# Mamba layer inside a three-engine scan: rows of B and C fetched by DMA instead of made on TensorE, one quarter of the gate z made during the scan, inputs reordered

## The chip, the cores and the metric

The program runs on one core of one Trainium2 chip. The metric is the device time of one execution in microseconds (us), the median of several runs. Names of engines: PE is TensorE, DVE is VectorE, ACT is ScalarE, POOL is GpSimd, SP is SyncE, which only issues DMAs here.

## The reference

Eight images of 512 patches with a class token ahead of them (513 tokens, 256 features) pass through two layers: attention with a diagonal state-space block and a quantised FFN with a depthwise convolution, then a Mamba block and a quantised gated FFN. The change touches only the Mamba block. With x the normalised input it computes, per image:

```
xv = silu(causal_conv4(W_in[:512] x) + b);  z = W_in[512:] x          # 512 channels, 513 tokens
dt = softplus(W_dt x[:64] + b_dt);  B = W_B x;  C = W_C x              # B, C: 16 rows each
for t:  h = exp(dt_t * A) * h + (dt_t * xv_t) * B_t                    # h: 512 channels x 16 states
        y_t = sum over the 16 states n of h[:, n] * C_t[n]
out = x + W_out (y * silu(z))
```

## The kernel before

Images go in pairs: PAIR = 2 images at a time, TURNS = 4 turns of a hardware loop. Features lie on the 128 partitions and tokens along the free axis, in f32. Each engine has its program written out by hand, with semaphores between them (`sem.wait_ge`), so the order on an engine is the order of the code.

A Mamba stage of one turn has three parts.

**Preparation.** After `layer_norm(3)`, PE makes the products `d` (for dt), `bc` (B and C), `x` and `z`, each 128 channels x 513 tokens (`fill`, L626), in four PSUM slots that are taken in turn; the slot of the product four places back must have been read (`slot_free`, table `readers`). ACT adds biases, makes Abs, Exp and Ln of the softplus and the first tap of the convolution; DVE makes three more taps for each of the 8 tiles (L1438), the rounding step `affine2(big4, mid4)`, and `dt_ready` (L1444); POOL makes the middle of the softplus (L1609, L1612) and dt times x (`dtx_ready`, L1616) for both images. DVE also splits `bc` into three bf16 parts `bcp` (L1414 to L1423), so that a bf16 matmul can spread a row exactly.

**Scan.** 32 steps k, 16 for each image: one state n of all 512 channels (4 tiles of 128 x 512, tokens 1 to 512; token 0 is done apart). Buffers `st(0, k)` hold the input of the scan and then h (3 buffers), `st(1, k)` hold h times C (2 buffers), both in the SBUF tensor `big`. In a step:

- PE spreads row B over the 128 partitions into the PSUM bank `b_psum`, and row C into `c_psum` (L852);
- DVE multiplies 3 tiles (even k) or 2 tiles (odd k) of dt*x, in SBUF, by B out of PSUM (`spread`, L1455); ACT copies the B row to SBUF, and POOL multiplies the other 1 or 2 tiles by that copy (`spread_pool`, L1623);
- ACT makes exp(dt*A) for each tile into one of two PSUM banks (`a_psum`);
- DVE scans the four tiles (L1504: decay from PSUM, input from SBUF);
- POOL multiplies all four tiles of h by row C (L1634, SBUF by SBUF), and PE adds the product into `y_psum` by a matmul with the identity (`add_y`, L873).

Order on DVE: `spread(k + 1)`, then the four scans of k. Order on POOL: the product with C of k (L1634), then `spread_pool(k + 2)`. `hc_ready` tells that the product with C is done, `scanned` that a tile is scanned, `y_summed` that PE has read `st(1, k)`.

**End.** The last step is split between DVE and POOL, `gated` multiplies y by silu(z), and PE projects with `wout`.

Of the kernel before, what the change touches and what calls it, by code (L numbers as in the profile page):

```python
# [23 lines left out]
P = 128  # L24
# [36 lines left out]
SETUP_POOL = 6  # L61
# [29 lines left out]
GU_ORDER = ["G0", "G1"] + [n for c in range(HT - 2) for n in (f"G{c + 2}", f"U{c}")] + [f"U{HT - 2}", f"U{HT - 1}"]  # L91


def plan_fills():
# [32 lines left out]
    each(*[f"d{c}" for c in range(DT)])  # L127
    each("bc")
    each(*[f"x{c}" for c in range(DT)])
    each(*[f"z{c}" for c in range(DT)])  # L130
# [47 lines left out]
def build(nc, x, w, scratch, out):  # L178
    with ExitStack() as ctx:
# [19 lines left out]
        wbc = sb("wbc", [P, KT, 96])  # L199
# [3 lines left out]
        sel = sb("sel", [96, 32], BF16)  # L203
        ones96 = sb("ones96", [96, P], BF16)
        bc0 = sb("bc0", [96, PAIR, 32], BF16)
# [15 lines left out]
        bcp = sb("bcp", [96, PAIR, T + 1], BF16)  # L221
# [35 lines left out]

        def big_un(p):
            o = p * 2 * W8
            return big[:, o:o + KT * T].rearrange("p (c t) -> p c t", c=KT)  # L260

        def big_sq(p):
            o = p * 2 * W8 + KT * T
            return big[:, o:o + KT * T].rearrange("p (c t) -> p c t", c=KT)

        def big4(p, n):
            o = p * 2 * W8 + 2 * KT * T + n * DT * T
            return big[:, o:o + DT * T].rearrange("p (c t) -> p c t", c=DT)

# [30 lines left out]
        def c_row(i):  # L300
            o = 5 * W4 + (i % 2) * S
            return big[:, o:o + S]

        def b_row(i):
            o = 5 * W4 + 2 * S + (i % 2) * S
            return big[:, o:o + S]
# [33 lines left out]
        c_psum = psum[:, 6 * BANK:7 * BANK]  # L340
        b_psum = psum[:, 7 * BANK:8 * BANK]

        def a_psum(j):
            o = (4 + j % 2) * BANK
            return psum[:, o:o + BANK]
# [66 lines left out]
        bc_split = signal("bc_split")  # L412
# [6 lines left out]
        b_spread = signal("b_spread")  # L419
        c_spread = signal("c_spread")  # L420
# [5 lines left out]
        c_copied = signal("c_copied")  # L426
        b_used = signal("b_used")
        b_copied = signal("b_copied")
# [48 lines left out]
        for p in range(PAIR):  # L477
# [23 lines left out]
            for c in range(DT):  # L501
                readers[f"x{c}", p] = (m_tap, 3 * (DT * p + c) + 3)
                readers[f"z{c}", p] = (z_silu, DT * p + c + 1)
                readers[f"d{c}", p] = (sp_pre, DT * p + c + 1)
            readers["bc", p] = (bc_split, 6 * p + 2)
# [10 lines left out]
        def _(sp):  # L516
# [17 lines left out]
            def turn(i, last):  # L534
# [41 lines left out]
                for g in range(NGRP):  # L576
                    stack_max(g)
                    if 1 <= g <= NG:
# [4 lines left out]
                        stack_quarter(g - 1, k_stack, K_PARTS, 2)  # L583
                if not last:
                    sp.wait_ge(q_ready, 4 * PAIR)
                    load_x(i + 1)
# [18 lines left out]
        def _(pe):  # L605
# [3 lines left out]
            with pe.Fori(0, TURNS) as i:  # L609
# [220 lines left out]
                for p in range(PAIR):  # L830
                    pe.wait_ge(ln_normed, q_of(3, p))
                    for c in range(DT):
                        fill(f"d{c}", p, [(wdt[:, c * P:(c + 1) * P], big_un(p)[:, 0])])
                for p in range(PAIR):
                    fill("bc", p, [(wbc[:, k], big_un(p)[:, k]) for k in range(KT)], rows=96)
                for p in range(PAIR):
                    for c in range(DT):
                        fill(f"x{c}", p, [(wx[:, k, c * P:(c + 1) * P], big_un(p)[:, k]) for k in range(KT)])
                for p in range(PAIR):
                    for c in range(DT):  # L840
                        fill(f"z{c}", p, [(wz[:, k, c * P:(c + 1) * P], big_un(p)[:, k]) for k in range(KT)])


                pe.wait_ge(z_silu, DT * PAIR)
                pe.wait_ge(bc_split, 6 * PAIR)
                pe.wait_ge(bc_first, 1)
                nc.tensor.matmul(c_psum[:, 0:PAIR * 32], ones96[:, :], bc0[:, :, :].rearrange("p b r -> p (b r)"),
                                 start=True, stop=True).then_inc(first_full, 1)

                def spread_row(k, r, o):  # L850

                    return nc.tensor.matmul(o, sel[:, r:r + 1].broadcast_to([96, P]), bcp[:, k // NS, 1:T],  # L852
                                            start=True, stop=True)

                def spread_b(k):
                    if k:
                        pe.wait_ge(b_copied, k)
                    spread_row(k, k % NS, b_psum).then_inc(b_spread, 1)

                def spread_c(k):  # L860
                    if k:
                        pe.wait_ge(c_copied, k)
                    else:
                        pe.wait_ge(first_copied, 1)
                    spread_row(k, NS + k % NS, c_psum).then_inc(c_spread, 1)
# [11 lines left out]
                spread_b(0)  # L877
                spread_c(0)
                spread_b(1)
# [21 lines left out]
                pe.wait_ge(c_copied, NS * PAIR)  # L901
                pe.wait_ge(b_copied, NS * PAIR)
                pe.wait_ge(tail_dve, DT - TAIL_DVE)
# [27 lines left out]
        def _(act):  # L931
# [11 lines left out]
            with act.Fori(0, TURNS) as i:  # L943
# [110 lines left out]
                for p in range(PAIR):  # L1054
                    for c in range(DT):
                        wait_full(act, f"d{c}", p)
# [662 lines left out]
```

## Time and profile before

| | us |
|---|---|
| median of 3 runs (2742.11 to 2752.42) | 2749.47 |
| the profiled execution, its own time | 2754.95 |
| its span, from the first to the last instruction | 2753.2 |
| DVE busy | 2053.7 (75%) |
| PE busy | 2143.3 (78%) |
| POOL busy | 1263.7 (46%) |
| ACT busy | 1289.8 (47%) |
| DMA, mean share of 16 engines, MB moved | 8.6%, 49.75 MB |

The span and what lies around it (1.8 us) make the execution's own time, which is 5.5 us above the median. The four turns repeat each other, so one turn is read in detail: the second one, in which the preparation runs from 1036.84 to 1088.18 us, the scan and its end from 1088.18 to 1303.62. Busy shares are averages over stages with different limits; the windows below say what fills one stage.

### The profile page before, as it was taken

To read this page: it belongs to the slowest core of one execution; us is meant where nothing else is said; L and a number is where in the kernel's file an instruction comes from. 1 tells how busy PE (TensorE), PEld (TensorE's weight loads), DVE (VectorE), ACT (ScalarE), POOL (GpSimd) and SP (SyncE) were. 2 spreads that over 40 slices of the span, in tenths; PEclk is the share of its full clock that TensorE was granted. 3 is DMA by queue.
4 is the path that set the end of the run, shared out by engine and by line. 5 is a ranking of instruction groups with operands and counts; after the bars stand their busy time and mean duration, and the time that the engine had idled before them with its cause. 6 is when DMAs were issued, how large, how long until landed. Compare 5 with 4: busy or idle time off the path is not lost.

```text
span 2753.2 us, 24356 instructions
## 1 busy us (share of the span) xinstructions
PE 2143.3 (78%) x8636; PEld 1147.9 (42%) x8676; DVE 2053.7 (75%) x2361; ACT 1289.8 (47%) x1822; POOL 1263.7 (46%) x615
## 2 busy tenths in 40 slices
PE   3988776677798877777779888677868989767786
PEld 1226662235422665223532376422443247532254
DVE  6844869986783487998678257899687827789957
ACT  1463356553164436654317443665323644455632
POOL 2130249991213025997222311799521231289932
PEclk9899998999999998899989999898998999989998
DMA  6300000000520000000051000000005100000000
GB/s 181 77 13 0 1 0 0 0 0 1 79 69 1 0 1 0 0 0 0 1 101 47 1 1 1 0 0 0 0 13 100 36 1 1 1 0 0 0 0 16
DMA packets 40562, 51.42 MB, mean 19 GB/s; under 512 B 8560, under 2 KB 31856, under 8 KB 40432
## 3 DMA queue, kind: packets, MB, share of 16 engines
q1 hardware_dynamic: 40432, 49.75, 8.6%
q8 instruction: 74, 1.21, 0.2%
q14 instruction: 56, 0.46, 0.1%
HBM read 26.25 MB, written 10.49 MB: 13 GB/s over the span
## 4 chain that ended last, share of the span: by engine, by line
PE 47%; DVE 22%; POOL 15%; issue 8%; ACT 5%; DMA 1%; SPq 0%; POOLq 0%; DVEq 0%; ACTq 0%
PE psum L626 14%; PE psum L873 12%; POOL big L1634 10%; PE psum L755 4%; POOL big L1623 4%; PE psum L730 4%; PE psum L743 3%; DVE mid L1209 3%; DVE mid L1438 3%; PE psum L688 2%; PE psum L699 2%; PE psum L767 2%; ACT mid L933 2%; PE psum L645 2%; DVE negmax L1309 2%
## 5 line engine op out<-in xcount | busy, mean ns | idle before, releaser
L873 PE MATMUL psum<-big,ident 128*128 128x512 f32 x992 | 527.2, 681 | 203.5 <-POOL big L1634 203.1
L1504 DVE TENSOR_TENSOR_SCAN big<-psum,b,big 128x512 f32<-128x512 f32 x512 | 613.4, 1256 | 0.0
L933 ACT ACTIVATE big<-psum 128x1024 f32<-128x1024 f32 (+2 forms) x592 | 452.4, 777 | 340.2 <-PE psum L743 206.2
L1634 POOL TENSOR_TENSOR big<-big 128x2048 f32<-128x2048 f32 x124 | 561.0, 4525 | 22.2 <-DVE big L1504 22.2
L933 ACT ACTIVATE psum<-mid,aneg 128x512 f32<-128x512 f32 x512 | 353.8, 692 | 265.0 <-DVE big L1504 265.0
L873 PEld LDWEIGHTS psum<-big,ident 128*128 128x128 f32 x992 | 203.1, 215 | 486.1 <-POOL big L1634 265.7
L1309 DVE TENSOR_REDUCE negmax<-psum 128x1 f32<-128x512 f32 x512 | 317.0, 677 | 15.8 <-PE psum L730 15.7
L1623 POOL TENSOR_TENSOR big<-mid,big 128x512 f32<-128x512 f32 (+1 forms) x128 | 223.7, 1748 | 19.9 <-ACT big L933 19.9
L730 PE MATMUL psum<-mid 96*128 96x512 bf16 x512 | 213.8, 421 | 23.0 <-DVE nm_rows L1325 13.2
L1577 POOL TENSOR_TENSOR lsum<-lsum,onorm 128x512 f32<-128x512 f32 x32 | 40.6, 1269 | 410.2 <-ACT onorm L933 410.2
L933 ACT ACTIVATE mid<-mid 128x513 f32<-128x513 f32 (+2 forms) x112 | 97.9, 899 | 228.4 <-DVE mid L1195 228.1
L743 PE MATMUL psum<-mid 99*128 99x512 bf16 x512 | 192.6, 396 | 12.4 <-DMA mid<-nm_rows 6.9
L1455 DVE TENSOR_TENSOR big<-mid,psum 128x1536 f32<-128x1536 f32 (+1 forms) x128 | 186.6, 1458 | 5.8 <-PE psum L852 5.7
L1599 POOL TENSOR_TENSOR big<-big,mid 128x513 f32<-128x513 f32 x40 | 51.5, 1300 | 287.5 <-ACT big L933 287.5
L933 ACT ACTIVATE mid<-psum 128x513 f32<-128x513 f32 x96 | 57.6, 600 | 234.7 <-PE psum L688 202.5
L1648 POOL TENSOR_TENSOR big<-big,mid 128x513 f32<-128x513 f32 x40 | 47.8, 1203 | 231.7 <-ACT big L933 231.3
L755 PE MATMUL psum<-big,mid 128*32 128x512 f32 x1024 | 135.6, 610 | 19.9 <-ACT osb L933 19.9
L633 PE MATMUL psum<-w 128*128 128x512 bf16 x568 | 131.8, 379 | 2.5 <-issue 0.6
L688 PE MATMUL psum<-ident,tok 128*128 128x128 f32 (+1 forms) x640 | 113.5, 327 | 25.1 <-DVE tok L1234 15.8
L730 PEld LDWEIGHTS psum<-mid 96*128 96x128 bf16 x512 | 51.1, 100 | 193.4 <-DVE negmax L1309 126.8
L852 PE MATMUL psum<-bcp,sel 96*128 96x512 bf16 x256 | 82.4, 399 | 59.3 <-ACT big L933 54.9
L933 ACT ACTIVATE mid<-psum,vec 128x513 f32<-128x513 f32 (+2 forms) x112 | 77.7, 713 | 98.4 <-PE psum L626 63.0
(170 smaller groups left out, 3466.9 us busy)
## 6 DMA issues: line engine op xcount, KB each, us to landing
mid<-mid SPq DMA_DIRECT2D x96, 128.0 KB, 8.8
mid<-scratch SPq DMA_DIRECT2D x192, 64.0 KB, 2.3
scratch<-big SPq DMA_DIRECT2D x4, 1536.0 KB, 14.4
out<-hres SPq DMA_DIRECT2D x8, 513.0 KB, 8.1
big<-in_x SPq DMA_DIRECT2D x8, 512.0 KB, 4.2
big<-in_w SPq DMA_DIRECT2D x2, 1024.0 KB, 6.4
mid<-nm_rows SPq DMA_DIRECT2D x96, 4.0 KB, 1.7
big<-in_wg SPq DMA_DIRECT2D x1, 1024.0 KB, 9.9
```

The lines of the kernel that those rows point to most:

```text
L626: mm = nc.tensor.matmul(o[:, a:b], lhs, rhs[:, a:b], start=(n == 0), stop=(n == len(products) - 1))
L688: mm = nc.tensor.matmul(o[:, t0:t0 + n], tok[0:n, p, which, c:c + 1].broadcast_to([n, P]), ident[0:n, 0:n], start=True, stop=True)
L730: nc.tensor.matmul(unit(("S", h, t)), q_stack[0:ROWS_MAX, h % H, t * P:(t + 1) * P], k_stack[0:ROWS_MAX, h % H, :], start=True, stop=True) ...
L743: mm = nc.tensor.matmul(st_unit(v)[:, t % 2], k_stack[0:KROWS, h % H, t * P:(t + 1) * P], q_stack[0:KROWS, h % H, :], start=True, stop=True)
L755: mm = nc.tensor.matmul(pv_bank[32 * j:32 * j + 32, :], vaug[:, g // NG, t, HG * (g % NG) + j], probs[:, g % 2, j, t], start=(t == 0), sto ...
L873: mm = nc.tensor.matmul(y_psum[:, c], ident[:, :], st(1, k)[:, c], start=(n == 0), stop=(n == NS - 1))
L933: return nc.scalar.activation(o, a, func, **kw)
L1309: V.tensor_reduce(negmax[:, h // HG % 2, k:k + 1], unit(("S", h, t)), AX_X, ALU.max, negate=True).then_inc(unit_free, 1)
L1455: V.tensor_tensor(st(0, k)[:, 0:m], mid4(k // NS, 3)[:, 0:m, 1:T], b_psum.unsqueeze(1).broadcast_to([P, m, S]), ALU.mult).then_inc(b_used, 1)
L1504: V.tensor_tensor_scan(st(0, k)[:, c], a_psum(DT * k + c), st(0, k)[:, c], b0[:, p, n, c:c + 1], ALU.mult, ALU.add).then_inc(scanned, 1)
L1623: G.tensor_tensor(st(0, k)[:, m:DT], mid4(k // NS, 3)[:, m:DT, 1:T], b_row(k).unsqueeze(1).broadcast_to([P, DT - m, S]), ALU.mult).then_in ...
L1634: G.tensor_tensor(st(1, k), st(0, k), c_row(k).unsqueeze(1).broadcast_to([P, DT, S]), ALU.mult).then_inc(hc_ready, 1)
```

## The change

Five things are changed:

1. **Rows by DMA.** `bc` is 32 rows in f32 and is no longer split. DVE copies it to SBUF (`bc_rows`), SP stores it to DRAM (`bc_dram`) and then loads each row of B and of C, 128 times over, into SBUF rows `b_row(k)` and `c_row(k)`, four of each (ROWS). `spread_b`, `spread_c`, `copy_b` and the copy of C are gone from PE and ACT. DVE's `spread` now reads the B row from SBUF, as POOL's does, and the last two products with C on DVE read it there too.
2. **z of image 1** is no longer filled ahead of the scan. Its four tiles are made in steps 3, 6, 9 and 12 of the scan (`Z_STEPS`) in a PSUM bank of their own, copied raw by ACT, and Silu is applied to all four after the last exponential. Token 0 of them is made ahead of the scan.
3. `a_psum` has three banks instead of two.
4. **Order of the inputs**: `MAMBA_FILLS` puts what belongs to image 0 first, and ACT and DVE follow it.
5. **dt times x of image 1** is made by DVE instead of POOL.

```diff
+MAMBA_FILLS = [(f"d{c}", 0) for c in range(DT)] + [("x0", 0), ("x1", 0)] + [(f"d{c}", 1) for c in range(DT)] \
+    + [("x2", 0), ("x3", 0), ("bc", 0), ("bc", 1), ("x0", 1), ("x1", 1), ("z0", 0), ("z1", 0), ("x2", 1), ("x3", 1),
+       ("z2", 0), ("z3", 0)]
+Z_STEPS = (3, 6, 9, 12)
+ROWS = 4
...
+        def b_row(k):
+            return row((6, 7, 0, 1)[k % ROWS])
+        def c_row(k):
+            return row((8, 9, 2, 3)[k % ROWS])
...
+        z_psum = psum[:, 7 * BANK:8 * BANK]
         def a_psum(j):
-            o = (4 + j % 2) * BANK
+            o = (4 + j % 3) * BANK
...
+                for p in range(PAIR):
+                    sp.wait_ge(bc_copied, p + 1)
+                    sp.dma_start(bc_dram[p], bc_rows(p)).then_inc(bc_stored[p], 16)
+                for k in range(PAIR * NS):
+                    p, n = divmod(k, NS)
...
+                    if k == 2:
+                        sp.wait_ge(bc_stored[1], 16)
+                        sp.wait_ge(dt_ready, PAIR)
+                    if k >= ROWS:
+                        sp.wait_ge(b_used, k - ROWS + 1)
+                        sp.wait_ge(b_pool, k - ROWS + 1)
+                    sp.dma_start(b_row(k), bc_dram[p, n:n + 1, 1:T].broadcast_to([P, S])).then_inc(b_in[k % ROWS], 16)
+                    if k >= ROWS:
+                        sp.wait_ge(hc_ready, k - ROWS + 1)
+                    sp.dma_start(c_row(k), bc_dram[p, NS + n:NS + n + 1, 1:T].broadcast_to([P, S])).then_inc(
+                        c_in[k % ROWS], 16)
...
+                def late_z(c):
+                    if c:
+                        pe.wait_ge(z_raw, c)
                     else:
                         pe.wait_ge(first_copied, 1)
+                        pe.wait_ge(z_first, 1)
+                    for k in range(KT):
+                        mm = nc.tensor.matmul(z_psum, wz[:, k, c * P:(c + 1) * P], big_un(1)[:, k, 1:T],
+                                              start=(k == 0), stop=(k == KT - 1))
+                    mm.then_inc(z_full, 1)
...
                 for k in range(PAIR * NS):
-                    if k + 2 < PAIR * NS:
-                        spread_b(k + 2)
-                    if k + 1 < PAIR * NS:
-                        spread_c(k + 1)
                     if k:
                         add_y(k - 1)
+                    if k in Z_STEPS:
+                        late_z(Z_STEPS.index(k))
...
-                            if j >= 2:
-                                act.wait_ge(scanned, j - 1)
+                            if j >= 3:
+                                act.wait_ge(scanned, j - 2)
                             run(a_psum(j), mid4(p, 2)[:, c, 1:T], ACT.Exp,
                                          scale=aneg[:, c * NS + n:c * NS + n + 1]).then_inc(decay, 1)
-                            if c == 1:
-                                if k >= 2:
-                                    act.wait_ge(hc_ready, k - 1)
-                                act.wait_ge(c_spread, k + 1)
-                                run(c_row(k), c_psum, ACT.Copy).then_inc(c_copied, 1)
-                                if k + 1 < PAIR * NS:
-                                    copy_b(k + 1)
+                            if c == 2 and k in Z_STEPS:
+                                zc = Z_STEPS.index(k)
+                                act.wait_ge(z_full, zc + 1)
+                                run(mid4(1, 1)[:, zc, 1:T], z_psum, ACT.Copy).then_inc(z_raw, 1)
+                nc.scalar.preload_act_table(ACT.Silu)
+                act.wait_ge(z_raw, DT)
+                for c in TAIL_ORDER:
+                    run(mid4(1, 1)[:, c, 1:T], mid4(1, 1)[:, c, 1:T], ACT.Silu).then_inc(z_late, 1)
+                load_ln_exp()
...
+                taps(0, 0)
+                taps(0, 1)
+                round_up(0)
+                taps(0, 2)
+                taps(0, 3)
+                for p in range(PAIR):
+                    copy_bc(p)
+                round_up(1)
+                taps(1, 0)
+                taps(1, 1)
+                steps_of(0)
+                taps(1, 2)
+                taps(1, 3)
+                steps_of(1)
                 dve.wait_ge(dt_ready, PAIR)
+                dve.wait_ge(m_silu, DT * PAIR)
+                V.tensor_tensor(mid4(1, 3), mid4(1, 2), mid4(1, 0), ALU.mult).then_inc(dtx_ready, 1)
 
                 def spread(k):
-                    dve.wait_ge(b_spread, k + 1)
+                    dve.wait_ge(b_in[k % ROWS], 16 * (k // ROWS + 1))
                     if k >= 3:
                         dve.wait_ge(hc_ready, k - 2)
                     m = b_dve(k)
                     V.tensor_tensor(st(0, k)[:, 0:m], mid4(k // NS, 3)[:, 0:m, 1:T],
-                                    b_psum.unsqueeze(1).broadcast_to([P, m, S]), ALU.mult).then_inc(b_used, 1)
+                                    b_row(k).unsqueeze(1).broadcast_to([P, m, S]), ALU.mult).then_inc(b_used, 1)
```

On DVE, a step in the middle of the scan stood like this before (L1455 is `spread`, the rows at L1504 are the scans, `mid` holds dt*x):

```order
L1455 TENSOR_TENSOR big<-mid,psum 128x1024 [waits hc_ready,b_spread]
L1504 SCALAR_TENSOR_TENSOR big<-psum,b,big 128x512 [waits decay,b_used]
L1504 SCALAR_TENSOR_TENSOR big<-psum,b,big 128x512 [waits decay] x2
L1504 SCALAR_TENSOR_TENSOR big<-psum,b,big 128x512 [waits b_pool,decay]
L1455 TENSOR_TENSOR big<-mid,psum 128x1536 [waits hc_ready,b_spread]
```

and stands like this now (`spread` is L1514, the scans L1566):

```order
L1514 TENSOR_TENSOR big<-mid,big 128x1024 [waits hc_ready,b_in3]
L1566 SCALAR_TENSOR_TENSOR big<-psum,b,big 128x512 [waits decay,b_used]
L1566 SCALAR_TENSOR_TENSOR big<-psum,b,big 128x512 [waits decay] x2
L1566 SCALAR_TENSOR_TENSOR big<-psum,b,big 128x512 [waits b_pool,decay]
L1514 TENSOR_TENSOR big<-mid,big 128x1536 [waits hc_ready,b_in0]
```

The sequence is the same; the second operand of `spread` has moved from `psum` to the SBUF tensor `big`.

On PE, steps 0 to 3 of the scan now read so (L910 is `add_y`, L900 is `late_z`, both in `psum`):

```order
L910 MATMUL psum<-big,ident 128x512 [waits hc_ready]
L910 MATMUL psum<-big,ident 128x512 x3
L910 MATMUL psum<-big,ident 128x512 [waits hc_ready]
L910 MATMUL psum<-big,ident 128x512 x3
L910 MATMUL psum<-big,ident 128x512 [waits hc_ready]
L910 MATMUL psum<-big,ident 128x512 x3
L900 MATMUL psum<-big,wz 128x512 [waits z_first,first_copied]
L900 MATMUL psum<-big,wz 128x512
```

The first product for z stands behind the third `add_y`, that of step 2, which waits for POOL's product with C of step 2. On ACT the same place reads (rows with `aneg` are the exponentials, the row with `z_full` the copy of z):

```order
L963 ACTIVATE psum<-mid,aneg 128x512 [waits dt_ready]
L963 ACTIVATE psum<-mid,aneg 128x512 x2
L963 ACTIVATE psum<-mid,aneg 128x512 [waits scanned] x12
L963 ACTIVATE mid<-psum 128x512 [waits z_full]
L963 ACTIVATE psum<-mid,aneg 128x512 [waits scanned] x12
```

The fourth exponential of step 3, and all behind it, stand after a copy that waits for PE's `late_z`.

## Rows read from the trace of the kernel before

**Rows 1.** Windows: length, busy us PE, PEld, DVE, ACT, POOL; PE clock, DMA share, GB/s.

```profile
1036.84:1088.18 51.34, 42.25 (x179) 33.70 (x179) 35.82 (x50) 33.64 (x41) 30.04 (x6) 0.95 0.00 0
1088.18:1303.62 215.44, 152.62 (x339) 61.41 (x340) 201.67 (x168) 123.42 (x192) 195.40 (x65) 0.89 0.00 0
```

**Rows 2.** Timeline of DVE over two steps: start, us, instructions.

```profile
1133.80 1.72 DVE L1455 TENSOR_TENSOR big<-mid,psum 128x1536 f32<-128x1536 f32 x1
1135.44 4.80 DVE L1504 TENSOR_TENSOR_SCAN big<-psum,b,big 128x512 f32<-128x512 f32 x4
1140.16 1.19 DVE L1455 TENSOR_TENSOR big<-mid,psum 128x1024 f32<-128x1024 f32 x1
...
1147.64 4.79 DVE L1504 TENSOR_TENSOR_SCAN big<-psum,b,big 128x512 f32<-128x512 f32 x4
```

**Rows 3.** Timeline of POOL over the same two steps.

```profile
1135.08 4.50 POOL L1634 TENSOR_TENSOR big<-big 128x2048 f32<-128x2048 f32 x1
1139.55 1.28 POOL L1623 TENSOR_TENSOR big<-mid,big 128x512 f32<-128x512 f32 x1
...
1145.26 2.20 POOL L1623 TENSOR_TENSOR big<-mid,big 128x1024 f32<-128x1024 f32 x1
1147.40 4.52 POOL L1634 TENSOR_TENSOR big<-big 128x2048 f32<-128x2048 f32 x1
```

**Rows 4.** Lines of DVE: count: ns shortest/median/longest, first and last start.

```profile
L1504 DVE TENSOR_TENSOR_SCAN big<-psum,b,big x512: 1245/1252/1278, 413.3 to 2633.1; 128x512 f32<-128x512 f32 x171
L1381 DVE TENSOR_TENSOR big<-psum,mid x24: 676/688/698, 281.7 to 2336.4; 128x513 f32<-128x513 f32 x24
L1387 DVE SCALAR_TENSOR_TENSOR big<-big,vec x32: 739/862/1804, 283.9 to 2338.3; 128x512 f32<-128x512 f32 x32
L1478 DVE TENSOR_TENSOR bxc<-first x8: 160/1311/2480, 405.4 to 2432.2; 128x16 f32<-128x16 f32 x8
L1201 DVE TENSOR_TENSOR mid<-mid x24: 1218/1226/1231, 227.2 to 2668.7; 128x1026 f32<-128x1026 f32 x24
```

**Rows 5.** Timeline of DVE and POOL at the end of the preparation.

```profile
1075.88 2.28 DVE L1444 SCALAR_TENSOR_TENSOR mid<-mid,big 128x2052 f32<-128x2052 f32 x1
1076.04 6.51 POOL L1616 TENSOR_TENSOR mid<-mid 128x2052 f32<-128x2052 f32 x1 [2.23 <-DVE mid L1444]
1082.52 4.50 POOL L1616 TENSOR_TENSOR mid<-mid 128x2052 f32<-128x2052 f32 x1
1084.59 2.54 DVE L1478 TENSOR_TENSOR bxc<-first 128x16 f32<-128x16 f32 x2 [6.43 <-ACT first L933]
```

**Rows 6.** Timeline of POOL and DVE in the first FFN of the same turn.

```profile
962.02 2.32 POOL L1599 TENSOR_TENSOR big<-big,mid 128x513 f32<-128x513 f32 x2 [61.42 <-ACT big L933]
963.10 1.79 DVE L1387 SCALAR_TENSOR_TENSOR big<-big,vec 128x512 f32<-128x512 f32 x1 [1.50 <-ACT big L933]
964.30 1.72 POOL L1599 TENSOR_TENSOR big<-big,mid 128x513 f32<-128x513 f32 x1
```

**Rows 7.** Timeline of PE and ACT in the scan: sums of y, an exponential.

```profile
1139.63 5.40 PE L873 MATMUL psum<-big,ident 128*128 128x512 f32 x8 [2.48 <-POOL big L1634]
1151.97 3.70 PE L873 MATMUL psum<-big,ident 128*128 128x512 f32 x8 [2.49 <-POOL big L1634]
1133.91 0.69 ACT L933 ACTIVATE psum<-mid,aneg 128x512 f32<-128x512 f32 x1 [0.49 <-DVE big L1504]
```

**Rows 8.** Preparation: a step of the chain that ended last; timeline of POOL and DVE.

```profile
1073.40 8.93 PE psum L626 x40
...
1060.06 4.54 POOL L1612 TENSOR_TENSOR big<-big 128x2052 f32<-128x2052 f32 x1
1072.60 0.75 DVE L1438 SCALAR_TENSOR_TENSOR mid<-psum,vec,mid 128x510 f32<-128x510 f32 x1
```

**Rows 9.** DMA issues: KB each, median us from issue to landing.

```profile
mid<-scratch SPq DMA_DIRECT2D x192, 64.0 KB, 2.3
wq<-in_wq SPq DMA_DIRECT2D x1, 256.0 KB, 14.0
```

More of the change, by code:

```diff
@@ L126, in plan_fills @@
     ln(3)
[L127 to L130, printed above, removed]
+    while len(order) % 4 != 2:
+        order.append(None)
+    order.extend(MAMBA_FILLS)
     while len(order) % 4 != 2:
@@ L411, in build @@
         z_silu = signal("z_silu")
-        bc_split = signal("bc_split")
+        z_first = signal("z_first")
+        z_full = signal("z_full")
+        z_raw = signal("z_raw")
+        z_late = signal("z_late")
+        bc_copied = signal("bc_copied")
+        bc_stored = [signal(f"bc_stored{p}") for p in range(PAIR)]
+        b_in = [signal(f"b_in{n}") for n in range(ROWS)]
+        c_in = [signal(f"c_in{n}") for n in range(ROWS)]
         sp_pre = signal("sp_pre")
@@ L850, in spread_row, with mamba_input @@
[L850 to L862, printed above, removed]
+                def mamba_input(name, p):
+                    kind, c = name[0], int(name[-1]) if name != "bc" else 0
+                    if kind == "d":
+                        fill(name, p, [(wdt[:, c * P:(c + 1) * P], big_un(p)[:, 0])])
+                    elif kind == "b":
+                        fill(name, p, [(wbc[:, k], big_un(p)[:, k]) for k in range(KT)], rows=2 * NS)
+                    else:
+                        wt = wx if kind == "x" else wz
+                        fill(name, p, [(wt[:, k, c * P:(c + 1) * P], big_un(p)[:, k]) for k in range(KT)])
@@ new lines, in _, with silu_z @@
+                absolute(0)
+                first_tap(0, 0)
+                first_tap(0, 1)
+                exponential(0)
+                for c in range(DT):
+                    step_input(1, c)
+                logarithm(0)
+                first_tap(0, 2)
+                absolute(1)
+                first_tap(0, 3)
+                exponential(1)
+                first_tap(1, 0)
+                logarithm(1)
+                nc.scalar.preload_act_table(ACT.Silu)
+                def silu_z(c):
@@ L1441, in _, with round_up, taps @@
-                for p in range(PAIR):
+                def round_up(p):
+                    dve.wait_ge(sp_act, 3 * p + 2)
+                    affine2(big4(p, 1), mid4(p, 3), 1.0, 1.0, ALU.add, ALU.subtract).then_inc(sp_round, 1)
+                def taps(p, c):
+                    k = DT * p + c
+                    dve.wait_ge(m_tap0, k + 1)
+                    xp, acc = slot(f"x{c}", p), mid4(p, 0)[:, c]
+                    for n in range(1, 4):
+                        if n > 1:
+                            dve.wait_ge(m_tap, 3 * k + n - 1)
+                        V.scalar_tensor_tensor(out=acc[:, n:T], in0=xp[:, 0:T - n], scalar=col("mw", 4 * c + 3 - n),
+                                               in1=acc[:, n:T], op0=ALU.mult, op1=ALU.add).then_inc(m_tap, 1)
```

206 lines of the change are left out of this document (82 added, 124 removed).

## Prediction

> **What bounds the kernel now.** I read the page first: DVE is busy for 75% of the span and POOL for 46%, which says little, because the four turns are made of stages with different limits. The chain of work that ended last shows that the scan is the longest stage with one pattern, so I read the windows of the second turn [rows 1]. From 1088.18 to 1303.62, 215.4 us, DVE is busy for 201.7 and POOL for 195.4. ACT has 123.4 and PE 152.6 of it. The timelines of two steps show it more sharply [rows 2, 3]. DVE starts the scans of a pair of steps at 1135.44 and the next pair at 1147.64: 12.20 us, with no idle time between `spread` and scans. POOL starts its product with C at 1135.08 and again, two steps on, at 1147.40: 12.32 us, also without idle time. So two engines bound the scan, each within 0.1 us of the other. Work taken off ACT and PE there gives nothing. Anything added to either bound engine is paid 16 times in a turn.
>
> The preparation takes 51.3 us, and there no engine is full: DVE has 35.8, PE 42.3, ACT 33.6, POOL 30.0 [rows 1]. The chain ends in the fills of z, 8.93 us of PE without a break [rows 8], after which the first state can be made, and in POOL's second product dt times x, which runs until 1087.02 [rows 5].
>
> **A resource that two engines share.** The rows show when DVE and POOL hold each other up. POOL's first L1616 took 6.51 us, the next, equal one 4.50; it was issued at 1076.04, while DVE's L1444 ran until 1078.16 [rows 5]. 1076.04 + 2.0 + 4.5 is 1082.5. The other way round: L1478 on DVE multiplies 16 elements and takes 160 ns at best, yet 2.48 us when it is issued at 1084.59 under a POOL product that ends at 1087.02 [rows 4, 5]. L1387 takes 739 ns at best and up to 1804 [rows 4]. All of these DVE instructions read two operands in SBUF. Those with one operand in PSUM are not touched by POOL: the 512 scans lie between 1245 and 1278 ns although POOL runs all the time beside them, and L1381 between 676 and 698 [rows 4]. So in this kernel a DVE instruction with two SBUF operands and a POOL product exclude each other, from start to end.
>
> The Trainium skill says it as a rule, in SBUF — State Buffer, section "Who interferes with whom": a DVE instruction with two SBUF inputs contends with a GpSimd instruction that reads SBUF, the one that starts second is blocked until the first is through, and one with at most one SBUF input isn't. The trace agrees: 6.51 us against 4.50. This rule speaks against the change; by a reading of the scan that left it out, DVE's part would cost the same 1.72 us as now.
>
> Who goes first when both wait? At 963.10 DVE asks while POOL starts the second of two products; a third POOL product is issued at 964.30 [rows 6]. DVE's row ends at 964.89 and POOL's third at 966.02, 1.72 long instead of some 1.1: the waiting DVE instruction went ahead of POOL's next one. So a wait lasts to the end of one instruction of the other. The handover is a little quicker than the sum of the rows: 964.89 less 0.74 is 964.15, 0.19 before the second product ended; L1478 ended at 1087.07, less 0.16 is 1086.91, 0.11 before POOL's end [rows 4, 5]. I take 0.15 a handover, between 0 and 0.3.
>
> **1. Rows by DMA, `spread` out of SBUF.** What is removed, two bf16 matmuls a step on PE and two copies on ACT, is beside the bound. What is added is that `spread` has both operands in SBUF. Its own length hardly changes: 1.19 us for 1024 elements, 1.72 for 1536 [rows 2], and 1.226 for 1026 elements with both operands in SBUF [rows 4]. But it now takes its time from POOL too. POOL has no gap to give: for two steps it needs 12.32, and DVE's two spreads hold it off for 1.19 + 1.72 = 2.91 less four handovers of 0.15, 2.3. The pair of steps becomes 14.6 us instead of 12.3. DVE waits too, for what POOL has begun, but it has 14.6 - 12.2 = 2.4 us a pair for that. 31 steps are 15.5 pairs: 36 us; I take 35, since the pause of DVE ahead of image 1, where it waits for y, lets POOL catch up. Bounds: no quick handover, 44; handovers of 0.3, 26.
>
> The transfers: 64 a turn of 256 KB. The bounds from rows are 2.3 us (64 KB out of DRAM) and 14.0 us (256 KB, queued behind other loads) [rows 9]. A row's buffer is free when step k-4 is done and is needed about three steps later, 22 us at the new pace. Even 14.0 lies within this, so I cost them at nothing. The first rows are stored and loaded 15 us or more before the scan; the rows of steps 2 and 3 wait for `dt_ready`, and are needed some 10 us later.
>
> **2. z in the scan.** The four tiles are cheap on PE (half of a `add_y` each, 1.85 us at the faster level [rows 7]). The place is not cheap. Count from the end of the last scan of step k-1, for k = 3, 6, 9, 12. DVE does `spread(k + 1)`, 1.2 to 1.7 with its wait 2, and three scans, 3.5: at 5.3 it needs the fourth exponential. On ACT that exponential stands behind the copy of z, the copy behind `late_z` on PE, that behind `add_y(k - 1)`, and that behind POOL's product with C of k-1. This begins when POOL is through with the spread it has in hand and with DVE's, at 2.2 (between 1.1 and 3.3), takes 4.5 [rows 3], `add_y` 4.5 (3.70 or 5.40 [rows 7]), z 1.9, the copy and the exponential 0.6 + 0.7 [rows 7]: 14.4. DVE stands for 9.1 us. POOL is behind by then and catches up some 1.8 of it, so one place costs 7.3 and the four 29 us a turn. The third bank of `a_psum` holds no more than one exponential, and does not help. Bounds: `add_y` at 3.70 and POOL beginning at 1.1 give 24, at 5.40 and 3.3 give 37.
>
> The four Silus come after the last exponential, while two scans, two products and the sums of y are still to be done: nothing.
>
> **3. Preparation.** Worked through with today's durations. The first tap starts at 1043 instead of 1051, since `x0` and `x1` are filled ahead of image 1's `d`. But PE now waits for slots, `bc` is filled only at about 1053 to 1056.5, and image 1's rounding stands behind its copies on DVE: 1059.4. POOL's two products for it take 4.5 each [rows 8], until 1069.7. In this time DVE's `steps_of(0)`, two SBUF operands, has been ready since about 1065.4, and waits until 1069.7. Then 2.3 [rows 5], six taps 4.5 [rows 8], `steps_of(1)` 2.3, dt times x 2.3, the small ones 1.0: the first `spread` starts at 1082.0. Before it was 1088.2, so 6 us a turn come back. Bounds: 10, if little waits, and 3.
>
> **Sum.** A turn: +35 + 29 - 6 = +58; four turns +232. 2754.95 + 232 = 2987; less the 5.5 us by which the profiled execution lies above the median, 2981; I say 2980. Bounds of this case: 4 x (26 + 24 - 10) = 160 and 4 x (44 + 37 - 3) = 312, so 2910 to 3062.
>
> **Rivals.**
> - *The exclusion costs, the z places don't*, say because ACT runs far enough ahead. Against it: ACT is held by `scanned`, three tiles ahead at most, and needs its fourth exponential 9 us before z is there. 4 x (35 - 6) = +116: 2865. 12%.
> - *The places of z cost, the exclusion doesn't*, because a row repeated over tiles is read otherwise. Nothing in the trace is like it; L1201 also repeats a row, but POOL is idle then. The preparation would gain 8: 4 x (27 - 8) = +76, 2825. 5%.
> - *Faster.* Neither holds: POOL's products slide into DVE's gaps, and the preparation's 8 us remain. 2749.5 - 32 = 2717. It decides where `spread` delays POOL by less than 0.25 us a step and z by nothing. Against it stands 6.51 against 4.50. 5%.
> - *Much slower*: POOL, running back to back, keeps DVE out until it has nothing to do. Then two steps take 14 us and another scan of 6.3, 20.3 instead of 12.3: 8 x 15.5 x 4 = +496 and with z and the preparation about 3340. The row at 964.30 speaks against it. Here too belongs the case that the DMAs set the pace: with 8 us for the two rows of a step instead of 7.3, it adds 87 to the forecast, 3067. Together 6%.
>
> The forecast itself has 72%. With the first rival it makes 84%, less the ends: the range is 2850 to 3060. Within 0.5% is what a measurement of this kernel can hardly tell from no change; only a chance meeting of gains and stalls would land there, 1%. Faster 5%, slower 94%.
>
> **What would show it.** In the new profile the lines of `spread` (L1514) should reach from 1.2 to some 4 us instead of 1182 to 1755 ns, POOL's product with C (L1689) should spread upward from 4.5 to about 6, and the scans stay at 1.25. A pair of steps should take 14.6 us. In steps 3, 6, 9 and 12 DVE should stand idle for about 9 us ahead of the fourth scan, released by ACT, and ACT by PE. The window of the preparation should be 45 us, with `steps_of(0)` at 4 to 6 us instead of 2.3. The loads of rows should land in 2 to 5 us and end no wait. If L1514 stays at 1.2 and 1.7 us, the part on the exclusion is wrong; if the stall of z is under 3 us, the count of the queue is wrong.

## The result, and the profile after

The changed kernel takes 2982.78 us (median of 4 runs, 2982.05 to 2985.21), the kernel before 2747.28 beside it: a ratio of 1.0857, with a 95% interval of 1.0838 to 1.0875. It is slower by 8.6%, and the forecast was 2980.

The windows of the second turn show the stages. The first row is the preparation, from the start of DVE's normalisation (L1253) to the first `spread`; the second is the scan, to the end of the last scan instruction on DVE. The columns are those of [rows 1].

```profile
1088.93:1137.32 48.39, 35.30 (x165) 27.64 (x162) 37.89 (x43) 33.83 (x42) 24.68 (x7) 0.91 0.18 46
1137.32:1401.70 264.38, 150.77 (x256) 58.27 (x256) 229.03 (x162) 90.52 (x133) 224.53 (x61) 0.80 0.21 56
```

For the kernel before, the windows cut at the same instructions are these:

```profile
1035.62:1088.18 52.56, 42.71 (x182) 33.70 (x179) 37.04 (x50) 34.13 (x42) 30.04 (x6) 0.95 0.00 0
1088.18:1289.15 200.97, 139.58 (x302) 53.85 (x302) 197.71 (x162) 123.42 (x192) 191.57 (x63) 0.90 0.00 0
```

(The preparation in [rows 1] begins one instruction later and so is 1.2 us shorter.) The scan went from 201.0 to 264.4 us, and the preparation from 52.6 to 48.4. The other turns differ by less than 1 us from these. DVE and POOL are "busy" longer in the scan by 31 and 33 us, although neither has more to do: the time in which an instruction is held off counts as busy, as the rows below show. ACT has 33 us less work there and PE 46 matmuls less, and neither makes the scan any shorter.

What held them off is to be seen in the lines of DVE and POOL (ns shortest/median/longest), beside [rows 4] and 1182/1468/1755 ns for `spread` (L1455) before, 4492/4520/4583 for POOL's product with C (L1634):

```profile
L1514 DVE TENSOR_TENSOR big<-mid,big x128: 1199/2032/3497, 400.2 to 2852.1; 128x1536 f32<-128x1536 f32 x64, 128x1024 f32<-128x1024 f32 x64
L1689 POOL TENSOR_TENSOR big<-big x124: 4514/5506/6032, 407.9 to 2860.6; 128x2048 f32<-128x2048 f32 x124
L1566 DVE TENSOR_TENSOR_SCAN big<-psum,b,big x512: 1249/1253/1284, 403.0 to 2862.3; 128x512 f32<-128x512 f32 x171
```

The shortest of each is nearly what it was (1199 against 1182, 4514 against 4492). The medians of the two that read only SBUF have grown, while the scans, with their decay in PSUM, are untouched. The timelines of DVE and POOL over a pair of steps without z answer to [rows 2, 3]:

```profile
1308.22 3.47 DVE L1514 TENSOR_TENSOR big<-mid,big 128x1536 f32<-128x1536 f32 x1
1311.62 4.80 DVE L1566 TENSOR_TENSOR_SCAN big<-psum,b,big 128x512 f32<-128x512 f32 x4
1316.34 2.03 DVE L1514 TENSOR_TENSOR big<-mid,big 128x1024 f32<-128x1024 f32 x1
1318.29 4.80 DVE L1566 TENSOR_TENSOR_SCAN big<-psum,b,big 128x512 f32<-128x512 f32 x4
...
1310.05 6.01 POOL L1689 TENSOR_TENSOR big<-big 128x2048 f32<-128x2048 f32 x1
1316.01 1.28 POOL L1678 TENSOR_TENSOR big<-mid,big 128x512 f32<-128x512 f32 x1
1317.24 5.49 POOL L1689 TENSOR_TENSOR big<-big 128x2048 f32<-128x2048 f32 x1
1322.70 2.17 POOL L1678 TENSOR_TENSOR big<-mid,big 128x1024 f32<-128x1024 f32 x1
1324.84 6.00 POOL L1689 TENSOR_TENSOR big<-big 128x2048 f32<-128x2048 f32 x1
```

Here both waits can be read. DVE's `spread` is issued at 1308.22, while POOL has its spread in hand until 1310.08; it runs from there and ends at 1311.69. POOL's product with C, issued at 1310.05, first waits for that and then takes its 4.5: 6.01. The pair takes 14.79 us (1310.05 to 1324.84) instead of 12.32.

In a step with z, DVE stands idle. The rows of DVE, POOL, PE and ACT in step 3 are, in the order in which they release each other:

```profile
1161.32 3.62 DVE L1566 TENSOR_TENSOR_SCAN big<-psum,b,big 128x512 f32<-128x512 f32 x3
...
1159.75 6.00 POOL L1689 TENSOR_TENSOR big<-big 128x2048 f32<-128x2048 f32 x1
...
1165.81 5.40 PE L910 MATMUL psum<-big,ident 128*128 128x512 f32 x8 [4.42 <-POOL big L1689]
1171.04 1.88 PE L900 MATMUL psum<-big,wz 128*128 128x512 f32 x4
...
1172.96 0.60 ACT L963 ACTIVATE mid<-psum 128x512 f32<-128x512 f32 x1 [14.25 <-PE psum L900]
...
1174.17 1.28 DVE L1566 TENSOR_TENSOR_SCAN big<-psum,b,big 128x512 f32<-128x512 f32 x1 [9.23 <-ACT psum L963]
1175.37 1.20 DVE L1514 TENSOR_TENSOR big<-mid,big 128x1024 f32<-128x1024 f32 x1
```

POOL's product with C of step 2 ends at 1165.75, `add_y` (L910) at 1171.2, z (L900) at 1172.9, ACT's copy at 1173.6; only then come the exponential and, at 1174.17, the fourth scan, 9.23 us after the third. In the whole program DVE waits 143.1 us for ACT in this place, 16 times. The last row is the next `spread`: POOL has nothing to do when it is issued, and it takes 1.20 us, as long as with its operand in PSUM. So an operand in SBUF, repeated over the tiles, does not slow DVE by itself.

The loads of the rows, 256 of them with 256 KB each, land 3.7 us after their issue in the median, and no wait on the page or in the scan ends with one.

### The profile page after: what moved, and what is told of

It is laid out like the page before. It is cut to its first block, busy times and chain, and to the rows that moved or that the text cites. A ratio compares the mean times of both kernels' runs of the same rounds, so it can differ in the third digit from the quotient of the medians.

```text
span 2980.9 us, 23769 instructions
## 1 busy us (share of the span) xinstructions
PE 2164.0 (73%) x8424; PEld 1147.0 (38%) x8424; DVE 2190.7 (73%) x2329; ACT 1165.1 (39%) x1594; POOL 1378.0 (46%) x607
## 4 chain that ended last, share of the span: by engine, by line
PE 32%; issue 26%; POOL 18%; DVE 17%; ACT 5%; DMA 1%; SPq 0%; POOLq 0%; DVEq 0%; ACTq 0%
POOL big L1689 12%; PE psum L660 11%; PE psum L789 4%; PE psum L764 3%; PE psum L777 3%; POOL big L1678 3%; ACT mid L963 3%; DVE mid L1261 3%; PE psum L733 2%; PE psum L722 2%; PE psum L801 2%; PE psum L679 2%; DVE mid L1194 2%; DVE negmax L1361 2%; DVE big L1307 2%
## 5 line engine op out<-in xcount | busy, mean ns | idle before, releaser
L910 PE MATMUL psum<-big,ident 128*128 128x512 f32 x992 | 603.8, 765 | 491.4 <-POOL big L1689 491.4
L1689 POOL TENSOR_TENSOR big<-big 128x2048 f32<-128x2048 f32 x124 | 706.1, 5694 | 163.1 <-DVE big L1566 163.1
L1566 DVE TENSOR_TENSOR_SCAN big<-psum,b,big 128x512 f32<-128x512 f32 x512 | 615.4, 1259 | 143.1 <-ACT psum L963 143.1
L910 PEld LDWEIGHTS psum<-big,ident 128*128 128x128 f32 x992 | 232.1, 246 | 859.6 <-POOL big L1689 593.6
L963 ACT ACTIVATE big<-psum 128x1024 f32<-128x1024 f32 (+1 forms) x336 | 304.1, 921 | 283.6 <-PE psum L777 202.8
L1514 DVE TENSOR_TENSOR big<-mid,big 128x1536 f32<-128x1536 f32 (+1 forms) x128 | 310.4, 2428 | 0.6
L963 ACT ACTIVATE mid<-psum 128x513 f32<-128x513 f32 (+2 forms) x100 | 57.7, 581 | 429.0 <-PE psum L900 211.8
L963 ACT ACTIVATE mid<-mid 128x513 f32<-128x513 f32 (+3 forms) x128 | 106.1, 865 | 218.1 <-DVE mid L1247 212.0
L667 PE MATMUL psum<-w 128*128 128x512 bf16 x608 | 139.2, 379 | 0.0
L722 PE MATMUL psum<-ident,tok 128*128 128x128 f32 (+1 forms) x640 | 117.3, 334 | 25.7 <-DVE tok L1286 16.2
L722 PEld LDWEIGHTS psum<-ident,tok 128*128 128x128 f32 (+1 forms) x640 | 105.0, 239 | 47.2 <-DVE tok L1286 23.4
L1261 DVE TENSOR_REDUCE mid<-big 128x513 f32<-128x4104 f32 x16 | 117.9, 7371 | 0.3
```

The lines of the kernel that those rows point to most:

```text
L722: mm = nc.tensor.matmul(o[:, t0:t0 + n], tok[0:n, p, which, c:c + 1].broadcast_to([n, P]), ident[0:n, 0:n], start=True, stop=True)
L910: mm = nc.tensor.matmul(y_psum[:, c], ident[:, :], st(1, k)[:, c], start=(n == 0), stop=(n == NS - 1))
L963: return nc.scalar.activation(o, a, func, **kw)
L1514: V.tensor_tensor(st(0, k)[:, 0:m], mid4(k // NS, 3)[:, 0:m, 1:T], b_row(k).unsqueeze(1).broadcast_to([P, m, S]), ALU.mult).then_inc(b_use ...
L1566: V.tensor_tensor_scan(st(0, k)[:, c], a_psum(DT * k + c), st(0, k)[:, c], b0[:, p, n, c:c + 1], ALU.mult, ALU.add).then_inc(scanned, 1)
L1689: G.tensor_tensor(st(1, k), st(0, k), c_row(k).unsqueeze(1).broadcast_to([P, DT, S]), ALU.mult).then_inc(hc_ready, 1)
```

## The experiments

The theory is that of the prediction: a DVE instruction with two SBUF operands and a POOL product exclude each other, and z stands in the wrong place of two queues. All edits below but that of run 4 are to the changed kernel. A ratio is to the kernel before, which took 2751.82 us beside runs 1 to 4 and 2752.88 beside runs 5 to 8.

**1. The z tiles in the same place on PE, copied later by ACT.**

```diff
-                            if c == 2 and k in Z_STEPS:
-                                zc = Z_STEPS.index(k)
+                            if c == 2 and k - 2 in Z_STEPS:
+                                zc = Z_STEPS.index(k - 2)
```

> The changed kernel, with ACT's copy of each z tile two steps later (steps 5, 8, 11, 14); PE makes z where it did. Theory (exclusion of DVE and POOL, and z's place): DVE's idle time ahead of the fourth scans of steps 3, 6, 9, 12 (143 us over the program, released by ACT) goes, the pairs of steps are all 14.8 us, and the time falls by 4 x 29 = 116 to about 2867. Rival (the DMAs of the rows slow the scan, and ACT's wait only shows it): over 2950.

2859.72 us, ratio to the kernel before 1.0401 (1.0359 to 1.0442). The window of the scan in the second turn:

```profile
1103.14:1337.14 234.00, 147.72 (x256) 57.37 (x256) 233.84 (x162) 91.30 (x133) 224.78 (x61) 0.82 0.24 63
```

No fourth scan waits any more, DVE is busy for 233.8 of 234.0 us, and the pairs of steps lie between 14.78 and 14.84 us (apart from the first and the one with the pause ahead of image 1). The place of z costs 30 us a turn (264.4 - 234.0), 123 in all by the medians. The DMAs are all there, so they aren't what makes DVE stand idle.

**2. Row B out of PSUM for DVE.** ACT copies each row of B that has come in by DMA into a PSUM bank, and DVE reads it there; for the bank, `a_psum` goes back to two.

```diff
+        b_psum = psum[:, 6 * BANK:7 * BANK]
-            o = (4 + j % 3) * BANK
+            o = (4 + j % 2) * BANK
...
+                def copy_b(k):
+                    act.wait_ge(b_in[k % ROWS], 16 * (k // ROWS + 1))
+                    if k:
+                        act.wait_ge(b_used, k)
+                    run(b_psum, b_row(k), ACT.Copy).then_inc(b_copied, 1)
...
+                            if c == 3 and k + 2 < PAIR * NS:
+                                copy_b(k + 2)
...
-                    dve.wait_ge(b_in[k % ROWS], 16 * (k // ROWS + 1))
+                    dve.wait_ge(b_copied, k + 1)
...
-                                    b_row(k).unsqueeze(1).broadcast_to([P, m, S]), ALU.mult).then_inc(b_used, 1)
+                                    b_psum.unsqueeze(1).broadcast_to([P, m, S]), ALU.mult).then_inc(b_used, 1)
```

> The changed kernel, with each B row copied by ACT out of its SBUF row into a PSUM bank, from which DVE's spread reads it; a_psum has two banks again, all DMAs stay, z stays in its place. Theory: with one operand in PSUM DVE no longer excludes POOL: spreads back to 1.19 and 1.72 us, POOL's product with C back to 4.5, a pair of steps without z 12.3 instead of 14.8; 4 x 34 = 136 less, about 2847, and the four idle stretches remain. Rival (DMA traffic into SBUF, which more than doubled, slows POOL and DVE): the pair stays above 14, time over 2940.

2857.15 us, ratio 1.0389 (1.0352 to 1.0426). The lines of `spread` (now L1527), the scans (L1579) and POOL's product with C (L1702):

```profile
L1527 DVE TENSOR_TENSOR big<-mid,psum x128: 1190/1472/1755, 404.7 to 2727.5; 128x1536 f32<-128x1536 f32 x64, 128x1024 f32<-128x1024 f32 x64
...
L1579 DVE TENSOR_TENSOR_SCAN big<-psum,b,big x512: 1249/1256/1285, 408.4 to 2736.8; 128x512 f32<-128x512 f32 x171
its engine sat idle before it (us, times) until:
  ACT psum L965: 136.1, 16
...
L1702 POOL TENSOR_TENSOR big<-big x124: 4498/4518/4548, 413.2 to 2734.9; 128x2048 f32<-128x2048 f32 x124
```

Both are back to their old lengths, with 117 MB of DMA beside them. Pairs of steps without z take 12.20 us. The idle time of DVE is still there, 136.1 us in 16 places. So what holds POOL and DVE up is where the second operand lies, and not the traffic. The scan is 233.9 us in the second turn: the exclusion costs 30.5 us beside the z places. The time is 10 us above what was expected, because the places of z cost more without the exclusion. Beside it, 124 of the 143.1 us of idle time are paid (the scans of the four turns against those of run 1), and the rest is caught up. Here, 134.5 of the 136.1 us are paid (against run 3).

**3. Both edits.**

> Both edits, the B row in PSUM for DVE and the later copy of z. Theory: the two costs are apart and add up: 4 x 65 = 260 less than the changed kernel, about 2724, a little under the kernel before by the shorter preparation (4 us a turn) and what else the change took off. Rival (one wait takes the place of the other, so the two share a cost): 2760 or more.

2726.77 us, ratio 0.9909 (0.9876 to 0.9943). The window of the scan:

```profile
1069.94:1270.14 200.20, 136.03 (x256) 53.50 (x256) 197.67 (x162) 105.81 (x163) 188.04 (x61) 0.87 0.28 74
```

The scan is as long as in the kernel before (200.2 against 201.0), and the preparation, 48.4 us, is still 4.2 shorter. The two costs add up to the whole of what the scan had lost: 264.4 - 200.2 = 64.2, of which z takes 30.4 beside the exclusion (run 1) and 33.7 without it (from 233.9 to 200.2). Taken away one at a time, the two give back 30.4 and 30.5, which is 3.3 less than both together.

**4. The exclusion alone, in the kernel before.** DVE's `spread` multiplies by `osb`, an SBUF row that lies there from the attention, instead of by row B in PSUM. This kernel leaves out row B for DVE's tiles, so it doesn't compute the layer; its instructions and waits are otherwise those of the kernel before.

```diff
-                                    b_psum.unsqueeze(1).broadcast_to([P, m, S]), ALU.mult).then_inc(b_used, 1)
+                                    osb[:, :].unsqueeze(1).broadcast_to([P, m, S]), ALU.mult).then_inc(b_used, 1)
```

> The kernel before, where DVE's spread multiplies by a fixed SBUF row instead of row B out of PSUM, and waits for all it waited for; the scan's input is thus another, everything else is done. No DMA is added. Theory: POOL and DVE exclude each other, a pair of steps takes 14.8 instead of 12.3: 2.5 x 15.5 x 4 = 155 more, about 2900. Rival (the cost comes from DMAs, from waits on them, or from the DMA'd rows): as before, 2750.

2887.17 us, ratio 1.0486 (1.0448 to 1.0524). The scan's window, and the timelines of DVE and POOL in it:

```profile
1115.91:1352.20 236.29, 159.89 (x302) 60.23 (x302) 234.68 (x162) 123.85 (x192) 228.44 (x63) 0.81 0.00 0
...
1197.88 3.49 DVE L1455 TENSOR_TENSOR big<-mid,osb 128x1536 f32<-128x1536 f32 x1
1201.30 4.79 DVE L1504 TENSOR_TENSOR_SCAN big<-psum,b,big 128x512 f32<-128x512 f32 x4
1206.01 2.06 DVE L1455 TENSOR_TENSOR big<-mid,osb 128x1024 f32<-128x1024 f32 x1
...
1197.56 2.20 POOL L1623 TENSOR_TENSOR big<-mid,big 128x1024 f32<-128x1024 f32 x1
1199.71 6.03 POOL L1634 TENSOR_TENSOR big<-big 128x2048 f32<-128x2048 f32 x1
```

One operand moved from PSUM to SBUF, without a DMA and without another wait, brings the same 3.5 and 2.05 us on DVE, the same 6.0 on POOL and the same pairs of 14.8 us. It costs 35.3 us a turn (236.3 - 201.0), and 135 in all by the medians. This is the cleanest of the runs.

**5. dt times x of image 1 back on POOL.**

```diff
-                dve.wait_ge(m_silu, DT * PAIR)
-                V.tensor_tensor(mid4(1, 3), mid4(1, 2), mid4(1, 0), ALU.mult).then_inc(dtx_ready, 1)
...
-                pool.wait_ge(dt_ready, 1)
-                pool.wait_ge(m_silu, DT)
-                G.tensor_tensor(mid4(0, 3), mid4(0, 2), mid4(0, 0), ALU.mult).then_inc(dtx_ready, 1)
+                for p in range(PAIR):
+                    pool.wait_ge(dt_ready, p + 1)
+                    pool.wait_ge(m_silu, DT * (p + 1))
+                    G.tensor_tensor(mid4(p, 3), mid4(p, 2), mid4(p, 0), ALU.mult).then_inc(dtx_ready, 1)
```

> The changed kernel, with dt times x of image 1 back on POOL. Theory: the preparation of a turn grows from 48.4 us (48.9 in some turns) by about 2.1, POOL's 4.5 for DVE's 2.3, to 50.5; 8 us in all, 2991. Rival (DVE's product has no worth, since POOL has time while DVE makes the last dt): 48.4, 2983.

2984.06 us (2979.16 to 2989.92), ratio 1.0838 (1.0809 to 1.0867). By the time alone this can't be told from the changed kernel; the intervals overlap. The profile can tell it: the preparation is longer, 50.66 us in the second turn against 48.39, and between 50.64 and 50.67 in all four, against 48.39 to 48.98.

```profile
1088.52:1139.18 50.66, 35.30 (x165) 27.65 (x162) 40.12 (x41) 33.84 (x42) 29.21 (x8) 0.89 0.15 44
```

The two lengths of the changed kernel go with TensorE's granted clock: from the start of the preparation PE comes to the fill of `bc` after 17.52 us where the granted clock in this stretch is 1.00 of full speed, and after 19.21 where it is 0.91. The first kind of turn lasts 48.4 us in the changed kernel, the second 49.0; 1.1 of the 1.7 us go into the wait of `steps_of(0)` for POOL, which is then 4.28 us long instead of 5.38. All four turns of run 5 are of the first kind. So like with like, this part of the change is worth 2.3 us a turn. The other 1.9 of the 4.2 us come from the new order of the inputs and from what left the preparation (the fills of z for image 1, the split of `bc`); no run tells these apart.

**6. DVE's taps of image 1, tile 2, ahead of `steps_of(0)`.**

```diff
-                steps_of(0)
                 taps(1, 2)
+                steps_of(0)
                 taps(1, 3)
```

> The changed kernel, with DVE's taps of image 1, tile 2, ahead of the addition that makes dt of image 0, which is ready but stands 3.1 us behind POOL's sum. Theory (exclusion from end to end): the taps fill that stretch, but the addition for image 1 then comes 2.3 us earlier into POOL's dt times x of image 0 and waits for its end; the preparation stays at 48.4 us and the time at 2983. Rival (DVE is merely slowed, not held off): 46.1 us a turn, 2974.

2982.18 us, ratio 1.0840 (1.0815 to 1.0865): no difference in the time, as expected. The timelines of DVE and POOL show why:

```profile
1116.50 2.29 DVE L1486 SCALAR_TENSOR_TENSOR mid<-mid,big 128x2052 f32<-128x2052 f32 x1
1118.71 2.32 DVE L1473 SCALAR_TENSOR_TENSOR mid<-psum,vec,mid 128x512 f32<-128x512 f32 x3
1120.94 4.61 DVE L1486 SCALAR_TENSOR_TENSOR mid<-mid,big 128x2052 f32<-128x2052 f32 x1
...
1118.87 4.52 POOL L1671 TENSOR_TENSOR mid<-mid 128x2052 f32<-128x2052 f32 x1 [3.27 <-DVE mid L1486]
```

The addition for image 0 is free of its wait (2.29 us, against 5.38 in the changed kernel), and the one for image 1 has it instead: issued at 1120.94, it takes 4.61, since POOL's product runs until 1123.39. Three of the turns show 50.0 us of preparation, 1.6 more than expected, and one 48.4. The three are turns with a granted clock of 0.91 up to the fill of `bc` (19.21 us), and the taps now stand in the wait that used to take up most of this; the fourth has 1.00 and takes 48.36, against 48.38 in the changed kernel. The rival of a mere slowing would have given 46.1.

**7. `late_z` ahead of `add_y` on PE**, ACT's copy left where it was.

```diff
-                    if k:
-                        add_y(k - 1)
                     if k in Z_STEPS:
                         late_z(Z_STEPS.index(k))
+                    if k:
+                        add_y(k - 1)
```

> The changed kernel, with late_z ahead of add_y on PE in steps 3, 6, 9 and 12; ACT's copy stays where it is. Theory: z no longer waits for POOL's product with C of the step before, so it is there before ACT's copy wants it; no idle time ahead of the fourth scans, about 2860 as with the later copy. Rival (the copy on ACT itself, or the switch of PE to other weights, costs the time): over 2900.

2875.65 us, ratio 1.0452 (1.0426 to 1.0478). Most of the idle time goes, though not all: in steps 6 and 12 the fourth scan still waits 3.9 and 2.5 us, because `late_z` stands behind `add_y(k - 2)` and this one behind POOL, which is late.

```profile
DVE big L1566 <- ACT psum L963: 25.8, 8, 3.9
```

That is 25.8 us in 8 places instead of 143.1 in 16. ACT's copy itself and the change of weights on PE are thus not the cost. But the order on PE isn't the whole of it either, and the time is 16 us above what was expected. The later copy on ACT (run 1) is the better cure, since it gives the whole queue two steps.

**8. The best of it.** The edits of run 3 and of run 6, and POOL's first two spreads only after DVE's small instructions for token 0.

```diff
                 pool.wait_ge(dtx_ready, PAIR)
+                pool.wait_ge(first_state, 3 * PAIR + 1)
                 spread_pool(0)
```

> B row in PSUM for DVE, later copy of z, taps of image 1, tile 2, first, and POOL's first two spreads only after DVE's small instructions for token 0, which in the changed kernel stand up to 2.1 us behind them. Theory: the preparation is 2 to 3 us a turn shorter than with the first two edits alone (48.4 us), 46 us; the scan stays at 200.2; about 2717, 1% under the kernel before. Rival (POOL's later start is paid back in the scan, POOL being a bound engine): 2727, as with the two edits.

2712.24 us (5 runs, 2711.67 to 2719.91), ratio 0.9860 (0.9839 to 0.9882): 1.4% less than the kernel before, a small difference but clear of the interval, and 9% less than the changed kernel. The windows of the second turn:

```profile
1016.94:1064.36 47.42, 36.98 (x165) 28.82 (x162) 34.08 (x43) 33.72 (x42) 21.26 (x5) 0.89 0.12 35
1064.36:1264.57 200.21, 132.36 (x256) 51.86 (x256) 197.67 (x162) 105.80 (x163) 191.44 (x63) 0.89 0.29 77
```

The small instructions at the end of the preparation no longer wait. In the changed kernel the rows of DVE are

```profile
1134.02 0.90 DVE L1548 TENSOR_TENSOR b<-mid,first 128x64 f32<-128x64 f32 x1
1134.84 2.14 DVE L1551 SCALAR_TENSOR_TENSOR mid<-mid,s 128x4 f32<-128x4 f32 x1
...
1133.57 3.39 POOL L1678 TENSOR_TENSOR big<-mid,big 128x512 f32<-128x512 f32 x2 [4.56 <-DVE mid L1506]
```

with POOL's two spreads beside them, and here

```profile
1063.62 0.26 DVE L1561 TENSOR_TENSOR b<-mid,first 128x64 f32<-128x64 f32 x1
1063.80 0.22 DVE L1564 SCALAR_TENSOR_TENSOR mid<-mid,s 128x4 f32<-128x4 f32 x1
...
1064.45 3.40 POOL L1691 TENSOR_TENSOR big<-mid,big 128x512 f32<-128x512 f32 x2 [5.84 <-issue]
```

The preparation is 45.8 us in the two turns with a granted clock of 1.00 up to the fill of `bc`, and 47.4 in the two with 0.91. All turns of run 3 are of the first kind and take 48.4, so the two last edits together are worth 2.6 us where the clock is the same, as expected; which of them gives how much was not run apart. POOL's later start costs nothing in the scan. By the medians run 8 is 14.5 us under run 3. The shorter preparations are 7.0 of this; the rest is not explained by the edits.

## Why the prediction was right

*What bounds the kernel.* Right. ACT and PE lost work in the scan, 33 us and 46 matmuls in a turn, and it makes nothing shorter. With DVE's operand and z's place mended (run 3) the scan is what it was, 200.2 us.

*The exclusion of DVE and POOL.* Right in mechanism, shown by run 4 alone, by run 2 the other way round, and by run 6 outside the scan. The term was 35 us a turn. Measured: 33.0 in run 1 (234.0 against 201.0), 35.3 in run 4. From the first scan of a turn to the start of the last pair the two agree, 34.5 and 34.7 us more than before. What differs is the start: from the first `spread` to the first scan the kernel before takes 4.3 us, the changed one and run 1 2.8, and run 4 4.9. The pair of steps was put at 14.6 and takes 14.79: the four handovers save 12.32 + 2.91 - 14.79 = 0.44 us, 0.11 each instead of 0.15. DVE's turn before POOL's next one, read from a single place [rows 6], holds for all of the 96 spreads (of 128) that had to wait in the changed kernel: none is longer than 3.5 us, which is a wait for one POOL spread and no more. The Trainium skill's rule (SBUF — State Buffer, "Who interferes with whom") is borne out in both halves: with two operands in SBUF a `spread` took up to 3.50 us (the changed kernel) and 3.51 (run 4), and with one in PSUM (run 2) neither engine is touched, 1755 ns at most for `spread` and 4548 for POOL's product.

*The place of z.* Right in mechanism: DVE waits for ACT, ACT for PE, PE for POOL. 9.1 us were worked out for one place; 9.2 are measured in 9 of 16, 7.53 to 9.99 in all. That the size came so near is partly luck, since both ends of the count were too early. Counted from the last scan of the step before, DVE needs the fourth exponential at 7.0 us in steps 3 and 9, where its `spread` is held off for 1.8 us, and at 5.5 in steps 6 and 12 (forecast 5.3 for all). In those 9 places the fourth scan starts at 16.2 and 14.7 (forecast 14.4), because POOL's product ends at 7.8 and 6.3 (forecast 6.7) and `add_y` takes 5.4 or more in 12 of 16 (forecast 4.5). Net of what POOL catches up z was put at 29 us a turn; it is 30.4. The lower bound of 24 doesn't follow from the prediction's own terms, which give 22. The title's "one quarter of the gate z" is also off: the tiles made in the scan are four of the eight of a turn.

*The preparation.* The sign was right, the size too large: 6 us forecast, 3.6 to 4.2 measured. Counted from the instruction where [rows 1] begins, the window is 47.2 us in the second turn instead of 45. The term that was mis-sized is "the small ones 1.0". They took 3.8 us from the end of dt times x (1133.50) to the first `spread` (1137.32), because POOL begins its first two spreads as soon as `dtx_ready` is there, and L1548 and L1551 stand behind them for 0.6 and 1.9 us. Up to the end of dt times x DVE was 0.7 us ahead of the forecast, since POOL's two products for image 1 took 3.82 us each instead of 4.5. It is the same exclusion, in a place where I counted DVE's instructions and not POOL's. Run 8 takes it away. The wait of `steps_of(0)`, forecast at "4 to 6 us instead of 2.3", was 5.38 in two turns and 4.28 in two.

*The DMAs.* Right: 3.7 us to landing, no wait.

*The sum.* The scan gives 4 x 64 = +256 and the preparation -16, together +240; the spans differ by 227.7. All but 1 of the missing 13 us lie in stretches that the change doesn't touch: ahead of the first turn's normalisation it is 5 us less (351.2 against 356.4), and the stretches between the end of the Mamba block and the next preparation are some us shorter or longer from kernel to kernel, without a change in their code. That 2980 came so near to 2983 owes something to these, which cancelled the sizes that were off. They are also why the 8 us that run 5's four preparations are longer can't be seen in its median.

## What to carry to other kernels

Where DVE and GpSimd both run near full, look at where each DVE operand lies before anything is moved: one operand in PSUM kept 2.5 us out of each pair of steps here, and moving a single operand to SBUF cost 5% of the program. ScalarE, which had time, can put a row that a DMA brought into PSUM; one such copy took 0.58 us in run 2. A product made "in the gaps" of a loop must be read where its queue leaves it, not where it is wanted: behind `add_y` it waited for another engine's work of the step before, and held up what stood behind its copy; taking it out of the bank two steps later gave back 123 us for two changed numbers.

## What was not expected of the hardware

POOL's products in the preparation became shorter in one image. L1609 took 4551/5009/5462 ns before (5.45 in image 0, 4.56 in image 1); the same product on the same 2052 elements, with its tile moved to another address of `big`, now reaches down to 3821:

```profile
L1665 POOL TENSOR_TENSOR big<-mid,big x8: 3821/4174/4562, 365.4 to 2575.6; 128x2052 f32<-128x2052 f32 x8
L1668 POOL TENSOR_TENSOR big<-big x8: 3817/4192/4569, 370.1 to 2579.5; 128x2052 f32<-128x2052 f32 x8
```

The four short ones of each line are those of image 1, whose tiles `big4(1, n)` lie elsewhere than before; image 0's, which didn't move, take 4.54. The address is the only difference that was found; no run changes it alone, so that it is the cause is not shown.

TensorE's granted clock, a mean over its two levels of 1.2 and 2.4 GHz, was 0.90 of full speed in the scan before and 0.80 in the changed kernel, where it stands idle for longer between the sums of y, and 0.89 again in run 8. `add_y` took 3.7 us or 5.1 to 5.4 in most steps of every kernel, and up to 6.8 in some. Outside the steps with z its only waits in the scan are those of DVE's `gate` of image 0, 7.3 us in four places of the kernel before and none in the changed one.
